# An attention block on one core: the beginning and the first unit rebuilt, with the parts of keys and queries staged in pieces

## The reference, cut to what matters

```python
n = layernorm(x)
latent = (n @ Wk + n @ Wv) @ W_down_kv            # 32 columns
q, k, v = n @ Wq, latent @ W_up_k, latent @ W_up_v
scores = (q_h @ k_h.T) / (sqrt(128) + 1e-8)       # per head, 1024 x 1024, clipped at +-10000
scores = scores * exp(-0.0001 * abs(i - j))       # decay with the distance of the rows
x = x + (softmax(scores) @ v_h, heads side by side) @ Wo
y = fp8_round(bfloat16(layernorm(x)) / s_in) @ fp8_round(kernel / s_k) * (s_in * s_k)
x = x + (bfloat16(y) + bias)
```

## Time and profile before

| | us |
|---|---|
| median of 3 runs (561.72 to 563.85) | 562.56 |
| the profiled execution | 561.57 |
| its span | 559.7 |
| ACT busy | 488.4 (87%) |
| PE busy | 494.6 (88%) |
| DVE busy | 315.5 (56%) |
| POOL busy | 175.8 (31%) |

### The profile page before, as it was taken

The page is one execution under the profiler, slowest core; times in us unless marked ns, Lnnn a source line. Parts: engine busy times, 40 slices in busy tenths (PEclk is TensorE's granted clock), DMA queues, the critical chain, the costliest instruction groups (busy, mean ns, idle before and its releaser), DMA issues.

```text
span 559.7 us, 9346 instructions
## 1 busy us (share of the span) xinstructions
PE 494.6 (88%) x3469; PEld 115.1 (21%) x3469; DVE 315.5 (56%) x786; ACT 488.4 (87%) x529; POOL 175.8 (31%) x121
## 2 busy tenths in 40 slices
PE   1788769999998999989998999989999999999961
PEld 1321111122111221222111221222112212122220
DVE  5367335455656566545657666545556565456656
ACT  1457759989999999989999999989999999999941
POOL 2399500969010202978100204887100001000100
PEclk9979989999999999999999999999999999999995
DMA  6364799736797610347797500357897300100000
GB/s 207 113 221 154 234 212 200 198 119 232 190 247 155 143 44 6 116 157 280 171 239 161 116 7 6 141 176 255 192 224 165 85 6 7 27 17 1 1 19 22
DMA packets 45600, 73.76 MB, mean 132 GB/s; under 512 B 5808, under 2 KB 26992, under 8 KB 45424
## 3 DMA queue, kind: packets, MB, share of 16 engines
q1 hardware_dynamic: 44016, 72.40, 48.0%
q10 hardware_dynamic: 1536, 0.73, 0.5%
HBM read 35.40 MB, written 35.65 MB: 127 GB/s over the span
## 4 chain that ended last, share of the span: by engine, by line
PE 50%; ACT 26%; issue 8%; DVE 6%; POOL 6%; DMA 3%; SPq 1%; ACTq 0%; POOLq 0%; DVEq 0%
PE ps L757 26%; ACT probs L580 25%; PE ps L744 15%; PE ps L631 2%; DMA Qs<-qp_dram 2%; POOL sq L479 2%; POOL sq L481 1%; PE ps L635 1%; PE ps L668 1%; POOL parts L483 1%; DVE ps L974 1%; PE ps L663 1%; PE ps L640 1%; DMA qp_dram<-parts 1%; DVE stats L893 1%
## 5 line engine op out<-in xcount | busy, mean ns | idle before, releaser
L580 ACT ACTIVATE probs<-ps 128x1024 f32<-128x1024 f32 x512 | 480.1, 1059 | 34.7 <-DVE ps L974 23.4
L757 PE MATMUL ps<-probs,V 128*9 128x512 f32 x2048 | 269.5, 598 | 3.6 <-DVE V L1091 1.1
L974 DVE TENSOR_TENSOR ps<-ps,consts 128x256 f32<-128x256 f32 (+1 forms) x256 | 143.5, 565 | 174.4 <-PE ps L744 155.1
L744 PE MATMUL ps<-Qs,Ks 64*128 64x512 bf16 x960 | 175.8, 386 | 24.2 <-ACT probs L580 10.8
L744 PEld LDWEIGHTS ps<-Qs,Ks 64*128 64x128 bf16 x960 | 42.3, 93 | 287.3 <-ACT probs L580 264.6
L508 POOL TENSOR_TENSOR xs<-xs,magic 128x512 f32<-128x512 f32 x7 | 8.9, 1276 | 194.9 <-DVE magic L1034 194.9
L757 PEld LDWEIGHTS ps<-probs,V 128*9 128x9 f32 x2048 | 31.3, 88 | 83.7 <-issue 59.2
L982 DVE COPY pv_out<-ps 105x512 f32<-105x512 f32 x31 | 21.4, 691 | 24.5 <-PE ps L757 24.5
L472 POOL TENSOR_TENSOR X<-X,mv 128x512 f32<-128x512 f32 x7 | 7.3, 1042 | 80.0 <-DVEq L1149 71.0
L479 POOL TENSOR_TENSOR sq<-kT,decay 128x768 f32<-128x768 f32 x8 | 15.5, 1941 | 52.7 <-DVE kT L1083 42.5
L481 POOL TENSOR_TENSOR sq<-sq,parts 128x768 f32<-128x768 f32 (+1 forms) x16 | 31.6, 1974 | 1.3
(11 more groups left out here) (130 smaller groups left out, 263.5 us busy)
## 6 DMA issues: line engine op xcount, KB each, us to landing
Qs<-qp_dram SPq DMA_DIRECT2D x32, 512.0 KB, 9.2
qp_dram<-parts SPq DMA_DIRECT2D x16, 768.0 KB, 4.6
Ks<-kp_dram SPq DMA_DIRECT2D x32, 384.0 KB, 7.5
kp_dram<-parts SPq DMA_DIRECT2D x16, 576.0 KB, 4.2
qp_dram<-parts SPq DMA_DIRECT2D x8, 512.0 KB, 6.0
kp_dram<-parts SPq DMA_DIRECT2D x8, 384.0 KB, 4.7
X<-L_attn_x SPq DMA_DIRECT2D x4, 512.0 KB, 7.2
kt_dram<-kT SPq DMA_DIRECT2D x4, 512.0 KB, 10.3
```

The costliest lines, as they stand in the source:

```text
L580: nc.scalar.activation(probs[:, quad % RING, 2 * jp:2 * jp + 2, :].rearrange("p j n -> p (j n)"), ps_all[:, bank * CH:(bank + 2) * CH], AC ...
L744: last = nc.tensor.matmul(bank, Ks[half, g, jp, key_cols(v, kc)], Qs[half, g, jp, v, qh * CH:(qh + 1) * CH], start=True, stop=True)
L757: last = nc.tensor.matmul(pv[32 * j:32 * j + VW, :], V[:, unit // 2 * NB + kc, HG * j + g, :], probs[:, quad % RING, j, :], start=i == 0, ...
L974: nc.vector.tensor_tensor(own, own, factors, ALU.mult).then_inc(fixed, 1)
```

## The change

It does these things:

- **Weights.** Wk and Wv come in transposed from the host (this is the order in which the arrays are laid out, `_TURNED`), and PE folds them by two accumulating matmuls; the sum on DVE, PE's transposition and one copy by ACT go.
- **Loads.** The first sequence comes in two halves (`x_half`, `x_in[0]`). The constants and the decay factors are issued only once the five weights are there, and the second sequence once the factors are. Five loads move behind the fold on ACT's queue or to SP's.
- **PE and ACT at the start.** PE runs 9, 2 and 7 matmuls on zeros into bank 0 (`keep_busy`); ACT computes one exponential of a constant before the first copy.
- **First unit.** One group in float32 instead of two (quads 0 to 7). `first_keys` and `first_queries` read the projections from PSUM. The slots begin after the first half's keys and queries; the second half's keys are projected after quad 0, its queries are a job at quad 5. DVE normalises both halves.
- **Parts in pieces.** Per sequence four pieces (early keys, early queries, late keys, late queries), five for sequence 0. Early pieces are what the first of the two units needs. Keys have one buffer of `parts`, queries the other; a piece is stored by three DMAs, as before a pair of them. `Qs` is laid out by unit first.
- **Order on SP.** For sequence 0: early keys 0 and early queries stored, loaded for group 1; early keys 1 stored and loaded for group 1 (`stage_more`, waited for at quad 12); groups 2 and 3 early; `store_qk`, rows; late keys and late queries stored; late pieces of groups 1 to 3 loaded (12 DMAs); `stage(0, 0)` (4 DMAs); then the loop, so `gather(0)` comes after all of it. For the other sequences the early pieces are stored behind `gather` of group 3, not ahead of it.
- **GpSimd.** `normalise` first computes the inverse deviations of the sequence itself, 14 dependent steps on 128 x 8 numbers, which DVE did in 12 (`prepare_rows`). The shift step goes from DVE's own list, which leaves 11. `keys`, `queries` become `early_parts`, `late_parts`.

```diff
-JOBS = [(0, "v", 0), (2, "v", 1), (26, "n", 0)]
+JOBS = [(FIRST_VALUES, "v", 0), (3, "v", 1), (5, "q", 1), (22, "n", 0)]
...
-        (14, "T", 0), (18, "T", 1), (22, "k", 0), (26, "k", 1), (28, "q", 0), (36, "q", 1), (38, "v", 0), (46, "v", 1))]
+        (14, "T", 0), (18, "T", 1), (22 if _b else 26, "k", 0), (26 if _b else 28, "k", 1),
+        (28 if _b else 30, "q", 0), (36, "q", 1), (38, "v", 0), (46, "v", 1))]
...
+            def store_keys(b, piece, to, at):
+                n = to.stop - to.start
+                sp.wait_ge(parts_ready, pieces_made(b, piece))
+                for j in range(STORED):
+                    rows = slice(PARTS * j, min(PARTS * j + PARTS, PRODUCTS))
+                    sp.dma_start(kp_dram[b, :, rows, to], parts[:, 0, j:j + 1, at:at + n]
+                                 .broadcast_to([P, rows.stop - rows.start, n])).then_inc(parts_out[0], 16)
...
+            early = slice(KL, KN)
+            early_keys = (slice(KL, 2 * KL), slice(2 * KL, KN))
+            store_keys(0, "early keys 0", early_keys[0], 0)
+            store_queries(0, "early queries", 0)
+            sp.wait_ge(parts_out[0], 16 * STORED)
+            sp.wait_ge(parts_out[1], 16 * STORED)
+            load_keys(0, 1, early_keys[0], stage_in[1])
+            load_queries(0, 1, slice(0, 1), stage_in[1])
+            store_keys(0, "early keys 1", early_keys[1], KL)
+            sp.wait_ge(parts_out[0], 16 * STORED * 2)
+            load_keys(0, 1, early_keys[1], stage_more)
+            for g in range(2, G):
+                load_keys(0, g, early, stage_in[g])
+                load_queries(0, g, slice(0, 1), stage_in[g])
             store_qk(0)
             load_x1(0)
             load_x1(1)
-            for which in range(2):
-                store_parts(0, which)
+            store_keys(0, "late keys", slice(0, KL), 0)
+            store_queries(0, "late queries", 1)
+            sp.wait_ge(parts_out[0], 16 * STORED * 3)
+            sp.wait_ge(parts_out[1], 16 * STORED * 2)
             for g in range(F32_GROUPS, G):
+                load_keys(0, g, slice(0, KL), stage_late[g])
+                load_queries(0, g, slice(1, 2), stage_late[g])
+            sp.wait_ge(qk_done, 2 * NB * F32_GROUPS)
+            for g in range(F32_GROUPS):
                 stage(0, g)
             for unit in range(UNITS):
                 b, qh = divmod(unit, 2)
                 for g in range(G):
                     group = unit * G + g
-                    if unit == 0 and g == F32_GROUPS:
-                        sp.wait_ge(qk_done, 2 * NB * F32_GROUPS)
-                        for first in range(F32_GROUPS):
-                            stage(0, first)
-                    if qh == 0 and g == 3 and b < B - 1:
-                        store_parts(b + 1, 0)
                     if qh == 1 and g == 0 and b < B - 1:
-                        store_parts(b + 1, 1)
+                        store_keys(b + 1, "late keys", slice(0, KL), 0)
+                        store_queries(b + 1, "late queries", 1)
                     if unit < UNITS - 1:
                         gather(group)
+                    if qh == 0 and g == 3 and b < B - 1:
+                        store_keys(b + 1, "early keys", early, 0)
+                        store_queries(b + 1, "early queries", 0)
...
             pool.wait_ge(decay_in, 16)
-            keys(0)
-            queries(0)
+            pool.wait_ge(k_sb, 1)
+            decayed_keys(PLUS, slice(0, 2 * P), 0)
+            decayed_keys(MINUS, slice(2 * P, CH), 2 * P)
+            split(0, CH, 0)
+            pool.wait_ge(q_sb, 1)
+            decayed_queries(0)
+            split(1, S, 0)
+            pool.wait_ge(k_sb, 2)
+            decayed_keys(MINUS, slice(CH, S), 0)
+            split(0, CH, CH)
+            normalise(1)
+            late_parts(0)
             squares(0)
...
+            act.wait_ge(tr_ps, 1)
+            nc.scalar.copy(xnT[:, 0:CH], ps[:, 4, :]).then_inc(xnT_ready, 1)
+            act.wait_ge(km0_ready, 2)
+            nc.scalar.copy(kT[:, 0:CH], ps[:, 5, :]).then_inc(k_sb, 1)
+            act.wait_ge(tr_ps, 2)
+            nc.scalar.copy(xnT[:, CH:S], ps[:, 7, :]).then_inc(xnT_ready, 1)
+            act.wait_ge(q0_ready, 2)
+            nc.scalar.copy(qT[:, 0:CH], ps[:, 6, :]).then_inc(q_sb, 1)
...
+            pe.wait_ge(tiles_clear, 1)
+            keep_busy(9)
+            pe.wait_ge(w_in, 32)
+            pe.wait_ge(fold_in, 48)
+            nc.tensor.matmul(ps[0:DL, 7, 0:D], wd_s[:, :], wkT_s[:, :], start=True, stop=False)
+            nc.tensor.matmul(ps[0:DL, 7, 0:D], wd_s[:, :], wvT_s[:, :], start=False, stop=True).then_inc(fold_pe, 1)
+            keep_busy(2)
             pe.wait_ge(fold_act, 1)
...
+            keep_busy(7)
...
             dve.wait_ge(decay_in, 16)
             dve.wait_ge(const_in, 16)
-            dve.wait_ge(k_sb, 1)
-            first_keys(0, PLUS, slice(0, 2 * P)).then_inc(km0_ready, 1)
-            dve.wait_ge(q_sb, 1)
-            first_queries(PLUS)
-            first_keys(0, MINUS, slice(2 * P, CH)).then_inc(km0_ready, 1)
-            first_queries(MINUS)
+            dve.wait_ge(k_ps, 1)
+            first_keys(0, PLUS, slice(0, 2 * P), ps[:, 5, 0:2 * P]).then_inc(km0_ready, 1)
+            first_keys(0, MINUS, slice(2 * P, CH), ps[:, 5, 2 * P:CH]).then_inc(km0_ready, 1)
+            dve.wait_ge(q_ps, 1)
+            first_queries(PLUS, ps[:, 6, :])
+            first_queries(MINUS, ps[:, 6, :])
```

```diff
+            def inverse_std():
+                var, y, y2 = [rs[:, k, :] for k in range(3)]
+                chain(nc.gpsimd.tensor_scalar(var, mv[:, :, 1], EPS, None, ALU.add))
+                chain(nc.gpsimd.tensor_scalar(y.bitcast(I32), var.bitcast(I32), -0.5, RSQRT_MAGIC, ALU.mult, ALU.add))
+                for _ in range(3):
+                    chain(nc.gpsimd.tensor_tensor(y2, y, y, ALU.mult))
+                    chain(nc.gpsimd.tensor_tensor(y2, y2, var, ALU.mult))
+                    chain(nc.gpsimd.tensor_scalar(y2, y2, -0.5, 1.5, ALU.mult, ALU.add))
+                    chain(nc.gpsimd.tensor_tensor(y, y, y2, ALU.mult))
...
+            def late_parts(b):
+                stored_before(b, 0, 2 if b == 0 else 1)
+                decayed_keys(PLUS, slice(2 * P, KP), 0)
+                split(0, KL, 0)
                 pool.wait_ge(q_sb, 2 * b + 2)
+                stored_before(b, 1, 1)
+                decayed_queries(1)
+                split(1, S, 0)
```

More of the change, by code:

```diff
@@ L47, in key_cols, with pieces_made, pieces_out @@
 def key_cols(v, kc):
-    at = kc * P if v == 0 else KP + (kc - 2) * P
+    at = KP + (kc - 2) * P if v == 1 else KL + kc * P if kc < 2 else (kc - 2) * P
     return slice(at, at + P)
+PIECES = ("early keys", "early queries", "late keys", "late queries")
+FIRST_PIECES = ("early keys 0", "early queries", "early keys 1", "late keys", "late queries")
+def pieces_made(b, piece):
+    if b == 0:
+        return FIRST_PIECES.index(piece) + 1
+    return len(FIRST_PIECES) + len(PIECES) * (b - 1) + PIECES.index(piece) + 1
+def pieces_out(b, which):
+    return 2 * b + (1 if which == 0 and b > 0 else 0)
 RSQRT_MAGIC = float(0x5F3759DF)
@@ L237, in build @@
         stage_in = [sem(f"stage_in{g}") for g in range(G)]
+        stage_more = sem("stage_more")
+        stage_late = [sem(f"stage_late{g}") for g in range(G)]
         sq_ready = sem("sq_ready")
@@ L353, in stage, with store_queries, load_keys @@
+            def store_queries(b, piece, qh):
+                sp.wait_ge(parts_ready, pieces_made(b, piece))
+                for j in range(STORED):
+                    rows = slice(PARTS * j, min(PARTS * j + PARTS, PRODUCTS))
+                    sp.dma_start(qp_dram[b, :, rows, qh * S:(qh + 1) * S],
+                                 parts[:, 1, 0:rows.stop - rows.start, :]).then_inc(parts_out[1], 16)
+            def load_keys(b, g, cols, count):
                 for i in range(2):
-                    rows = slice(64 * i, 64 * i + 64)
@@ L362, in store_qk, with stage @@
+            def stage(b, g):
+                for which in range(2):
+                    sp.wait_ge(parts_out[which], 16 * STORED * pieces_out(b + 1, which))
+                load_keys(b, g, slice(0, KN), stage_in[g])
+                load_queries(b, g, slice(0, 2), stage_in[g])
             def store_qk(b):
@@ L484, in split, with stored_before @@
+            def split(which, n, at):
+                r = rest[:, 0:n]
+                to = [parts[:, which, k, at:at + n] for k in range(PARTS)]
+                chain(nc.gpsimd.tensor_copy(to[0], r))
+                chain(nc.gpsimd.tensor_tensor(r, r, to[0], ALU.subtract))
+                chain(nc.gpsimd.tensor_copy(to[1], r))
+                chain(nc.gpsimd.tensor_tensor(to[2], r, to[1], ALU.subtract))
                 pool.sem_inc(parts_ready, 1)
-            def keys(b):
+            def stored_before(b, which, more):
+                pool.wait_ge(parts_out[which], 16 * STORED * (pieces_out(b, which) + more))
@@ L525, in _ @@
```

(9 more changed lines are left out.)

279 lines of the change are left out of this document (136 added, 143 removed).

## The result

The changed kernel is slower: 568.32 us (median of 16 runs, 565.3 to 573.2) against 563.51 us for the kernel before (16 runs, 561.4 to 568.0). The ratio is 1.0086, with a 95% interval from 1.0061 to 1.0111: a loss of under 1%, but clear of the noise. Forecast were 558.6 us, a range from 549.0 to 566.5, and faster as the likeliest of the three signs. Value and sign were both missed.

What follows compares the result with a forecast made beforehand. ACT's back-to-back exponentials, 0.964 us each, were taken to bound the kernel. +1.3 us up to number 53, -5.1 for three stalls and -0.2 at the end sum to -4.0: against the median 562.6, 558.6 us, range 549 to 566.5.

Steps and rivals of the forecast that it cites:

- where unit 0 stalls, and on what: First unit: ACT idles some 15 us from about 80, while DVE's pv_out copy waits for gather(0).
- T: Time at which gather(0) lands, taken as 95 us, uncertain by 4; the kernel's time moves with it one to one.
- Number 53: Exponential 53 on ACT, counted from 0, second of quad 26: forecast at 98.7 us, 1.3 later than before (97.35).
- let the gather pass: Rival at gather(0): the queue doesn't hold it, time 5.5 to 10.5 us under forecast, about 550.5; chance 0.15.
- the start: Steps up to POOL's first work, forecast at 15.1 us instead of 22.4; first exponential about 8 us earlier.
- The projection's gain: First key projection on PE at the start: 1.4 us saved if keep_busy acts like earlier work.
- number 17: Exponential 17 on ACT, counted from 0, starting 3.5 us after group 1 is loaded: forecast at 46.4 us.
- the restart: After gather(0) lands: DVE's copy, 0.7 us, and about 3 us to the second exponential, 3.7 together.
- the 14 steps on POOL: Inverse deviations moved to POOL: taken at 0.3 us each, costing nothing.
- What stays: After unit 0: moving the gather of group 3 ahead removes three stalls, -5.1 us; the end gives -0.2.
- Small pieces at the price of whole ones: Rival at the 12 late loads: small loads cost as whole ones; half the excess gives T = 102, 565.6 us; chance 0.17.
- No stall at all: Rival in quad 25: gather(0) is there when wanted, the 16.2 us lead stays, about 541 us; chance 0.08.

Runs made afterwards that it cites:

- experiment 2: Changed kernel with the 12 late loads ahead of gather(0) cut from 2304 KB to 288, full ones loaded behind it: 564.57 us, ratio 0.9994 to before.
- experiment 11: experiment 9 without the 18 matmuls on zeros at the start: 544.62 us, ratio 0.9656 to the kernel before.
- experiment 9: The edits of experiment 5 and experiment 6 together, on experiment 1: 542.35 us, ratio 0.9612 to the kernel before.
- experiment 3: Changed kernel with early keys and early queries of sequences 1 to 3 again stored ahead of the gather of group 3: 590.67 us, ratio 1.0437 to before.
- Experiment 13: Changed kernel, gather(0) left in place, early keys stored ahead of gather(3) and POOL's squares behind to_grid: 559.75 us, ratio 0.9917 to before.
- experiment 1: Changed kernel with gather(0) issued directly behind the store of the late queries, not in the loop: 551.47 us, ratio 0.9732 to the kernel before.
- experiment 7: experiment 1 without keep_busy, the 18 matmuls on zeros at the start: 552.92 us, ratio 0.98 to the kernel before.
- experiment 10: experiment 9 with the 11 inverse-deviation steps for the next sequence on DVE, two to a quad, not on POOL: 556.85 us, ratio 0.988 to before.
- Experiment 4: The kernel before with the gather of group 3 moved ahead of the next sequence's key stores, nothing else: 570.69 us, ratio 1.0085 to before.
- experiment 5: experiment 1 with POOL's squares of the next sequence moved behind to_grid: 544.34 us, ratio 0.9645 to the kernel before.
- experiment 6: experiment 1 with the early keys alone stored ahead of gather(3), early queries left behind it: 544.47 us, ratio 0.9667 to the kernel before.
- experiment 12: The kernel before with gather(3) ahead of the key stores and POOL's squares behind to_grid: 570.46 us, ratio 1.0124 to before.

## Why the prediction was wrong

**Right: where unit 0 stalls, and on what.** The forecast had ACT idle some 15 us from about 80, released by DVE, whose copy waits for `gather(0)`: 14.62 us from 83.7. The gather was to land at T = 95: 96.97. Number 53 at 98.7: 101.02. The queue served in order, as taken from the row load of the earlier trace rows: experiment 2 bears it out. The Trainium skill (DMA: Bandwidth & Descriptors, Queues, rings and completion order), whose rule would have let the gather pass, did not decide here: a gather issued up to 88.9 landed at 96.97.

**Off by about 2 us: the start.** POOL starts at 16.83 where 15.1 stood. The projection's gain was there (1.10 us, against 2.05 without the matmuls on zeros in experiment 11); the fold was late: ACT's copy of `wk_eff` is at 9.25 in the changed kernel's trace and at 7.82 in that of experiment 9, whose beginning is the same program. PE worked at half the pace, on the seven matmuls on zeros too, and the transpositions behind them began at 12.10 in place of 10.33. The changed kernel, then experiment 9:

```profile
9.14 3.17 PE L717 MATMUL ps<-xn 128*128 128x512 bf16 x7
```

```profile
7.71 1.68 PE L720 MATMUL ps<-xn 128*128 128x512 bf16 x7
```

This differs by execution and not by program. Of nine traces with this beginning POOL starts at 16.83 to 16.88 in three (the changed kernel, experiments 3 and 13), at 15.10 in one (experiment 1) and at 14.45 to 14.62 in five; without the matmuls (experiments 7 and 11) at 15.88 and 15.90. So `keep_busy` gained up to 1.4 us or lost 1.0, and the 15.1 was a fair middle. Early queries were made at 31.37 for 29.3, number 17 started at 49.24 for 46.4, late queries were made at 62.65 for 59.7 and stored by 72.90, when the loads behind them go out, for 71.5. T came 2.0 later than summed (of which the start may explain some 1.5: in experiment 2 POOL started 2.4 earlier, and the late loads went out 1.45 earlier), and the restart took 4.1 for 3.7. Number 53 is 2.3 later than forecast, within the uncertainty that I gave.

**Right: the 14 steps on POOL.** 0.20 us each, 0.28 with the wait, and no `late_parts` later for it: POOL's next wait, for its buffer at 48.31, still has 3.15 us. But "nothing" hid that the steps stand ahead of late parts which do matter: spread over DVE's quads, so that those parts came 10 us later, they cost 14.5 us (experiment 10).

**Wrong: "What stays", and so the sign.** The step reads "three stalls go, -5.1". They did go (`rec` waits 0.9 us in place of 5.5), and the stretch became 5.3 us longer. I had looked at what `gather(3)` waits behind and never at who waits behind the store that took its place. POOL does: early and late keys share a buffer, as the parts did before. That put up to 5.34 us on POOL's chain, and its instructions on DVE's small steps. Experiment 4 shows the move alone at +0.85% where I summed -0.9%. Experiments 5, 6 and 9 show the cause: with the overlap removed, the wait removed, or both, the stretch takes 401.3, 403.6 and 401.0 us where it took 410.6 in experiment 1. Experiment 13 shows the same with `gather(0)` in its place: 400.8 us, so that 3.6 of the 5.1 us are there, and 559.75 us in all.

**What I had no term for.** That a DVE step and a POOL instruction share something was priced nowhere, although had the sign of it: one normalising step took between 0.333 and 1.196 us with POOL on the same tile. The Trainium skill (SBUF — State Buffer, SBUF: two separate sides) has it as an exclusive lock on a port pair that DVE and GpSimd share, held for the whole instruction. The trace agrees: in three cases (269.17, 271.02 and, in experiment 12, 141.26) a small step ended within 0.03 us of the POOL instruction that it began beside, and `wide` in experiment 4 ended 0.55 after it (254.03, 253.48). By that rule a rival would have been due, slower than before, with POOL's phase as what decides.

**The rivals.** Small pieces at the price of whole ones fell: T = 96.97, not 102. The result landed near that rival's 565.6 for another reason, in another stage. No stall at all was no outcome of this program, and what it would be worth is shown by experiment 1: a ratio of 0.9732 in place of 1.0086, with every other edit of the change in place. Experiment 9, with the steady part mended too, measured 542.35 us; that rival was summed at 541.

**What is open.** Of the 4.8 us between the medians, the traces put 3.7 in unit 0, 5.3 behind it and 0.3 at the end, 9.2 in all and 4.4 too many. The excess is how far the two profiled executions lie from their medians (2.4 above, 1.9 under). The slow start of this execution is 2.3 us against five of the nine traces; how often it comes in runs without a profile was not measured. Nor was a third buffer for the parts tried in the kernel before, which might take POOL's wait away there with the gather left in front.

## What to carry to other kernels

An item that is moved in an in-order queue has two prices: what it no longer waits behind, and what its old neighbours now wait for. Follow the semaphore of each DMA that moves back to whoever reuses its buffer, and that engine's phase to what it then lies beside. When bulk transfers are put ahead in a queue, the small DMA behind which an engine blocks goes ahead of them: here eight of them, issued in time that SP spent waiting, turned a loss of 0.9% into a gain of 2.7%.

## What the runs showed of the hardware

- Beside a POOL instruction of 1.9 us, DVE's steps on 128 x 4 numbers took 1.60 and 1.82 us in place of 0.17, and beside one of 2.36 us a step with two operands of 128 x 512 took 2.73 in place of 0.69. DVE's steps on PSUM (`fix`, the `pv` copy) kept their 0.43 and 0.69 beside the same POOL work.
- The granted TensorE clock does not tell all. The first projection took 2.05 us in experiment 11 and 1.10 in experiment 9, and the clock reads 1.00 from 11 to 14 us in both. In experiment 1, where it took 1.55, the clock reads 0.63 in the microsecond from 12 and 0.50 in the next. The seven matmuls on zeros took 3.17 us in the changed kernel and 1.68 in experiment 9, with 1.00 read in both.
- In the long idle of the changed kernel, PE does nothing from 83 us on, and the clock fell to half, 1.2 GHz (1.00 until 85, 0.50 from 86). It was still there when the work came back, and reads 1.00 again from 103, with PE busy since 98. How much of the restart's 4.1 us this costs was not measured apart:

```profile
90.00:95.00 5.00, 0.00 (x0) 0.00 (x0) 0.00 (x0) 0.00 (x0) 0.00 (x0) 0.50 1.14 184
95.00:100.00 5.00, 2.19 (x10) 0.26 (x10) 1.30 (x2) 1.02 (x1) 0.00 (x0) 0.50 0.22 47
100.00:105.00 5.00, 5.00 (x26) 0.95 (x24) 2.09 (x3) 3.00 (x3) 0.00 (x0) 0.75 0.06 11
```

(Stretch, its length, busy time and count of PE, its weight loads, DVE, ACT and POOL, granted clock, DMA share, GB/s.)
